# Three tiles for rows of B in a Mamba and mixture-of-experts layer, with every step's place chosen anew

## What is computed

```python
h0 = layernorm(x)
xs, z = split(h0 @ in_proj_w.T)                    # 512 features each
xc = silu(causal_conv4(xs) + conv_b)
B, C, d = split(xc @ x_proj_w.T)                   # 16, 16 and 1 values a token
dt = softplus(d);  A = -exp(A_log)                 # A: 512 x 16
# over time, for each feature and each n of 16:
h[n] = exp(dt * A[:, n]) * h[n] + dt * B[n] * xc
y = sum_n C[n] * h[n]
x = x + ((y + D * xc) * silu(z)) @ out_proj_w.T
t = layernorm(x)
w, e = top2(softmax(t @ router_w.T + router_b))    # 2 of 8 experts
x = x + sum_k w[k] * (t @ expert_weights[e[k]])
```

## Time and profile before

| | us |
|---|---|
| median of 3 runs | 2778.48 |
| lowest and highest | 2769.5, 2797.36 |
| profiled execution, its own time | 2768.58 |
| its span, first to last instruction | 2766.5 |
| busy PE, DVE | 2313.6, 2273.5 |
| busy POOL, ACT | 1809.8, 1488.8 |

### The profile page before, as it was taken

One profiled execution on the slowest core, in us unless ns is written; L12 is line 12 of the kernel. 1 busy time (PEld: TensorE's weight loads), 2 busy tenths in 40 slices (PEclk: granted clock), 3 DMA queues, 4 the chain that ended last, 5 costly groups with the idle time before them and its releaser, 6 DMA issues.

```text
span 2766.5 us, 34600 instructions
## 1 busy us (share of the span) xinstructions
PE 2313.6 (84%) x9510; PEld 1336.4 (48%) x9510; DVE 2273.5 (82%) x3144; ACT 1488.8 (54%) x2417; POOL 1809.8 (65%) x1418
## 2 busy tenths in 40 slices
PE   5668777798979889798988889798987989798886
PEld 2435353554545454454545455454544545454432
DVE  3899999899899989898999979898899989888200
ACT  3554646465654746565564656556574656545221
POOL 2556767557576767768676766767686676669442
PEclk8878788799989999898999989899999999999998
DMA  3873412324233434435343444534444353456875
GB/s 121 277 264 95 155 59 58 96 77 134 73 122 112 138 118 116 132 111 145 114 146 103 123 132 109 145 104 148 115 121 128 105 155 107 126 153 183 217 209 152
DMA packets 192570, 366.27 MB, mean 132 GB/s; under 512 B 22912, under 2 KB 22912, under 8 KB 192384
## 3 DMA queue, kind: packets, MB, share of 16 engines
q1 hardware_dynamic: 144272, 263.26, 29.8%
q0 software_dynamic: 28672, 67.13, 11.3%
q10 hardware_dynamic: 19440, 33.69, 3.4%
HBM read 212.73 MB, written 151.26 MB: 132 GB/s over the span
## 4 chain that ended last, share of the span: by engine, by line
PE 33%; DVE 24%; POOL 15%; issue 14%; ACT 11%; DMA 2%; SPq 0%; DVEq 0%; POOLq 0%; another core or an unknown queue 0%; ACTq 0%
DVE h L1069 13%; PE bank L1240 12%; PE bank L1244 11%; POOL u L785 9%; PE bank L1255 7%; DVE acc L1077 6%; ACT bank L930 4%; PE bank L1235 3%; DVE xc L1100 2%; ACT L930 1%; ACT xc L982 1%; POOL row_scratch L872 1%; PE bank L1317 1%; POOL row_scratch L870 1%; POOL x_out L885 1%
## 5 line engine op out<-in xcount | busy, mean ns | idle before, releaser
L785 POOL TENSOR_TENSOR u<-xc,b_ring 128x1024 f32<-128x1024 f32 x512 | 1230.2, 2419 | 644.4 <-DVE h L1069 434.9
L930 ACT ACTIVATE bank<-dt,neg_a 128x512 f32<-128x512 f32 x1024 | 701.6, 689 | 799.4 <-DVE h L1069 686.4
L1255 PE MATMUL bank<-ident,h 128*128 128x128 f32 x4096 | 643.4, 292 | 240.5 <-DVE h L1069 137.5
L1255 PEld LDWEIGHTS bank<-ident,h 128*128 128x128 f32 x4096 | 511.2, 150 | 559.4 <-DVE h L1069 206.2
L1069 DVE TENSOR_TENSOR_SCAN h<-bank,h_last,u 128x512 f32<-128x512 f32 x512 | 652.7, 1276 | 93.8 <-ACT bank L930 52.6
L1077 DVE SCALAR_TENSOR_TENSOR acc<-bank,ct,acc 128x512 f32<-128x512 f32 x960 | 696.5, 726 | 7.7 <-PE bank L1255 7.5
L1069 DVE TENSOR_TENSOR_SCAN h<-bank,u 128x512 f32<-128x512 f32 x512 | 620.9, 1215 | 92.8 <-ACT bank L930 54.6
L1240 PE MATMUL bank<-w_exp,xeT 128*128 x764 | 381.6, 623 | 43.5 <-ACT xeT L1038 20.5
L1244 PE MATMUL bank<-w_exp,xeT 128*128 x764 | 362.1, 596 | 0.0
L1240 PE MATMUL bank<-xnT,w_in 128*128 128x512 f32 x512 | 257.4, 627 | 9.2 <-DVE acc L1077 3.6
L1244 PE MATMUL bank<-xnT,w_in 128*128 128x512 f32 x512 | 242.3, 596 | 0.0
(11 more groups left out here) (149 smaller groups left out, 2193.1 us busy)
## 6 DMA issues: line engine op xcount, KB each, us to landing
b_ring<-b_scratch SPq DMA_DIRECT2D x256, 256.0 KB
xe<-row_scratch SPq DMA_DIRECT2D x165, 256.0 KB
result_scratch<-ye SPq DMA_DIRECT2D x165, 256.0 KB
row_scratch<-x_out ACTq DMA_DIRECT2D x32, 1024.0 KB, 5.4
x<-in_x SPq DMA_DIRECT2D x66, 256.0 KB, 4.3
x_scratch<-x SPq DMA_DIRECT2D x64, 256.0 KB, 2.4
xn<-in_x SPq DMA_DIRECT2D x62, 256.0 KB, 3.7
x_out<-x_scratch SPq DMA_DIRECT2D x44, 256.0 KB, 4.6
```

Of the source, the lines that this page charges most:

```text
L785: nc.gpsimd.tensor_tensor(out=u[:, at:at + 2, :], in0=xc[:, half, 2 * k:2 * k + 2, :], in1=b_ring[:, n % ROWS:n % ROWS + 1, :].to_broadcas ...
L930: nc.scalar.activation(decay_bank(j, n, c)[:], dt[:, half, :], ACT.Exp, scale=neg_a[:, c, n:n + 1]).then_inc(decay_ready, 1)
L1255: last = nc.tensor.transpose(ps[:, k * P:(k + 1) * P], tile(k), ident[:])
```

## The change

ROWS goes from 2 to 3. The tile of a row is now chosen by its number over all blocks (16 rows don't divide by 3), in the request and in `u`. `load_b` leaves the head of the slots and becomes a step with a place of its own, in a new table B_ROWS, 15 for the rows of this pass and one for row 0 of the next block. All other tables have new places; the steps themselves and their waits are as they were. In the diff, lines of tables that the text doesn't name are left out.

```diff
--- before.py
+++ after.py
@@ -26,7 +26,7 @@
     BATCHES = TOKENS // SEQ
     LN_EPS = 1e-5
     EPS = 1e-10
-    ROWS = 2
+    ROWS = 3
     UR = 4
     XP = 2 * N + 1
     TOP = 2
@@ -60,123 +60,127 @@
     ROW_ZEROS = 32
 
     COMBINE = {
...
-        "gather": [8.8, 12.29, 29.08, 31.46, 41.89, 47.71, 54.7, 60.67],
...
+        "gather": [15.12, 17.05, 30.19, 32.14, 42.99, 48.01, 53.62, 60.57],
...
     }
     POST = {
-        "load_res": [2.18, 3.07, 4, 5.1],
-        "y_T": [4.43, 4.52, 4.87, 4.87],
-        "y_skip": [5.75, 5.85, 7.57, 7.79],
-        "y_gate": [6.67, 6.71, 10.4, 10.55],
-        "out_project": [10.75, 11.89, 14.71, 15.84],
...
-        "residual": [12.98, 15.77, 16.24, 18.77],
-        "rstd2": [19.16, 21.93],
...
-        "norm2": [18.17, 18.67, 22.72, 24.06],
...
-        "router": [18.97, 21.04, 25.63, 27.28],
...
-        "gate_weights": [37.72],
-        "rank": [35.14],
-        "row_of": [38.98],
...
-        "scatter": [48.38, 52.16, 59.82, 62.85],
+        "load_res": [1.66, 3.92, 8.45, 8.63],
+        "y_T": [4.81, 4.81, 4.83, 4.9],
+        "y_skip": [5.78, 5.9, 7.96, 8.28],
+        "y_gate": [8.01, 9.19, 10.19, 11.31],
+        "out_project": [10.75, 11.67, 12, 16.16],
...
+        "residual": [12.95, 14.45, 17.62, 19.91],
+        "rstd2": [18.09, 25.08],
...
+        "norm2": [19.53, 20.65, 24.77, 25.1],
...
+        "router": [19.37, 22.67, 26.41, 28.79],
...
+        "gate_weights": [38.47],
+        "rank": [38.34],
+        "row_of": [39.91],
...
+        "scatter": [49.1, 55.25, 59.55, 66.53],
     }
     PREP = {
-        "load_x": [0, 0.96, 8, 8.36],
...
-        "norm_apply": [10.01, 10.14, 18.01, 18.99],
-        "norm_T": [9.89, 9.9, 16.62, 17.49],
...
-        "silu_x": [38.14],
...
-        "xp_project": [38.68],
-        "xp_evict": [40.96],
...
-        "b_scale": [43.97],
-        "b_store": [50.38],
+        "load_x": [0, 3.7, 7.42, 8.24],
...
+        "norm_apply": [11.14, 11.43, 18.88, 19.14],
+        "norm_T": [10.02, 11.31, 18.31, 18.35],
...
+        "silu_x": [39.93],
...
+        "xp_project": [38.39],
+        "xp_evict": [42.44],
...
+        "b_scale": [48.39],
+        "b_store": [55.58],
     }
     EXPERTS = {
...
-        "rows_load": [6.06, 7.2, 8.67, 20.56, 28.6, 34.67, 38.35, 39.62, 47.1, 50.39, 60.45, 62.19],
...
-        "expert_end": [14.16, 16.45, 20.89, 28.62, 33.06, 35.44, 42.33, 49.08, 56.19, 60.91, 62.38, 68.25],
-        "expert_evict": [17.5, 19.88, 25.42, 34.04, 37.55, 39.98, 51.57, 57.23, 60.02, 64.58, 67.09, 71.31],
-        "rows_store": [17.96, 19.22, 34.78, 36.85, 38.91, 46.01, 53.05, 56.99, 61.37, 64.93, 65.49, 73.82],
...
+        "rows_load": [4.09, 6.76, 9.47, 18.9, 27.93, 30.67, 37.96, 43.43, 46.7, 50.29, 59.19, 60.15],
...
+        "expert_end": [14.75, 17.61, 21.83, 29.4, 34.15, 36.83, 43.33, 50.38, 56.79, 61.3, 62.43, 69.25],
+        "expert_evict": [18.43, 19.98, 24.15, 35.52, 38.95, 42.62, 53.13, 58.59, 60.46, 66.77, 68.73, 74.52],
+        "rows_store": [16.92, 19.51, 32.79, 39.28, 40.82, 55.88, 58.41, 59.3, 64.87, 67.3, 70.28, 73.12],
     }
     EXPERTS_LATE = {
-        "late_rows_load": [3.82, 4.26, 4.29, 4.39, 9.49, 12.64, 16.21, 17.84, 21.26, 25.9, 27.45, 29.91, 30.44, 37.02, 39.03, 42.58, 45.34, 46.59, 48.78, 53.56, 54.22, 56.16, 56.2],
-        "late_rows_T": [7.93, 9.04, 9.12, 11.54, 17.77, 18.54, 21.06, 21.53, 25.39, 27.97, 28.35, 31.68, 36.22, 38.05, 41.48, 44.27, 45.94, 50.51, 53.54, 55.96, 57.56, 59.45, 62.5],
...
+        "late_rows_load": [4.28, 4.32, 4.52, 4.87, 14.14, 15.01, 16.4, 16.83, 21.47, 24.84, 26.4, 26.99, 31.61, 33.1, 37.49, 39.73, 46.34, 47.29, 50.18, 54.92, 54.98, 55.47, 55.93],
+        "late_rows_T": [8.08, 9.09, 11.25, 13.25, 16.13, 17.77, 20.05, 21.53, 25.59, 26.08, 28.35, 32.67, 36.42, 38.05, 42.18, 43.44, 46.33, 50.51, 54.81, 55.12, 56.68, 58.01, 60.69],
...
     }
     EXPERTS_END = {
...
     }
     POST_END = {
-        "end_load_res": [0.7, 7.69, 8.52, 9.85],
...
-        "end_store_x1": [3.27, 9.96, 12.1, 15.35],
...
-        "end_rank": [47.69],
+        "end_load_res": [0.1, 1.7, 8.6, 8.77],
...
+        "end_store_x1": [2.97, 9.4, 10.55, 13.54],
...
+        "end_rank": [49.89],
         "end_row_of": [66.9],
...
         "end_scatter": [66.9, 66.9, 66.9, 66.9],
     }
     COMBINE_LATE = {
...
-        "near_gather": [56.5, 58.66, 60.91, 61.75, 63.81, 65.23, 66.3, 66.67],
...
+        "near_gather": [56.62, 58.74, 60.54, 64.14, 64.44, 65.21, 66.26, 66.9],
...
+    }
+    B_ROWS = {
...
     }
     PAIRS = [(i, k) for i in range(Q) for k in range(TOP)]
     INDEX = {"gather": PAIRS, "late": [(i, k) for k in range(TOP) for i in range(Q)], "conv": [(c, k) for c in range(C) for k in range(EDGE)]}
@@ -262,6 +266,10 @@
         side = combine_in(j) + post_in(j) + prepare_in(j) + experts_in(j)
         if j in NEW_GROUP:
             side = [(6, ("new_group", NEW_GROUP[j]))] + side
+        if scan:
+            side = side + [(at, ("load_b", n + 1, 0)) for n, at in enumerate(B_ROWS["load_b"])]
+        if do_prep:
+            side = side + [(B_ROWS["next_load_b"][0], ("load_b", 0, 1))]
         if j == 0:
             side = side + [(2 * i + 1, ("zero_rows", i)) for i in range(ROW_ZEROS)]
         if j == 1:
@@ -274,11 +282,6 @@
         steps = []
         for at in range(N * C):
             n, c = at // C, at % C
-            if c == 0:
-                if scan and n + 1 < N:
-                    steps.append(("load_b", n + 1, 0))
-                elif do_prep and n + 1 == N:
-                    steps.append(("load_b", 0, 1))
             if scan:
                 steps += [("u", n, c // 2)] * (c % 2 == 0) + [("decay", n, c), ("scan", n, c)]
             k = at - C - LAG
@@ -672,7 +675,8 @@
                         n, of = s[1], j + s[2]
                         sync.wait_ge(b_stored, 16 * (of + 1))
                         wait(sync, u_ready, (of * N + n - ROWS + 1) * C // 2)
-                        sync.dma_start(b_ring[:, n % ROWS, :], b_dram[(half + s[2]) % 2, n:n + 1, :].to_broadcast([P, T])).then_inc(b_loaded[n % ROWS], 16)
+                        row = of * N + n
+                        sync.dma_start(b_ring[:, row % ROWS, :], b_dram[(half + s[2]) % 2, n:n + 1, :].to_broadcast([P, T])).then_inc(b_loaded[row % ROWS], 16)
                     elif s[0] == "rows_load":
                         g, at, tile = tile_of(s[1])
                         if at == 0:
@@ -775,15 +779,16 @@
                         nc.gpsimd.tensor_tensor(out=shift1[:, two], in0=mean[:, two], in1=rstd[:, two], op=ALU.mult).then_inc(shift_ready, 1)
                     elif s[0] == "u":
                         n, k = s[1], s[2]
+                        row = j * N + n
                         if k == 0:
-                            pool.wait_ge(b_loaded[n % ROWS], 16 * (j * (N // ROWS) + n // ROWS + 1))
+                            pool.wait_ge(b_loaded[row % ROWS], 16 * (row // ROWS + 1))
                         if n == 0 and k == 0:
                             pool.wait_ge(xc_ready, (j + 1) * C)
                         g = n * 2 + k
                         at = 2 * (g % 2)
                         wait(pool, scanned, j * N * C + 2 * (g - 1))
                         nc.gpsimd.tensor_tensor(out=u[:, at:at + 2, :], in0=xc[:, half, 2 * k:2 * k + 2, :],
-                                                in1=b_ring[:, n % ROWS:n % ROWS + 1, :].to_broadcast([P, 2, T]), op=ALU.mult).then_inc(u_ready, 1)
+                                                in1=b_ring[:, row % ROWS:row % ROWS + 1, :].to_broadcast([P, 2, T]), op=ALU.mult).then_inc(u_ready, 1)
                     elif s[0] == "conv_edge" and half == 0:
                         base = j // 2 * EDGE_STEPS
                         if j == 0:
```

More of the change, by code:

```diff
@@ L62, in mamba_moe_kernel @@
     COMBINE = {
-        "fetch": [3.46, 12.94, 35.73, 39.01],
-        "gather": [8.8, 12.29, 29.08, 31.46, 41.89, 47.71, 54.7, 60.67],
-        "store": [27.39, 35.74, 61.02, 66.51],
+        "fetch": [4.82, 14.74, 38.7, 41.01],
+        "gather": [15.12, 17.05, 30.19, 32.14, 42.99, 48.01, 53.62, 60.57],
+        "store": [31.86, 34.91, 61.37, 66.64],
     }
     POST = {
-        "load_res": [2.18, 3.07, 4, 5.1],
-        "y_T": [4.43, 4.52, 4.87, 4.87],
-        "y_skip": [5.75, 5.85, 7.57, 7.79],
@@ new lines, in mamba_moe_kernel @@
+        "out_project_end": [10.81, 11.99, 14.14, 17.66],
+        "residual": [12.95, 14.45, 17.62, 19.91],
+        "rstd2": [18.09, 25.08],
+        "store_x1": [11.18, 13.47, 16.85, 18.99],
+        "norm2": [19.53, 20.65, 24.77, 25.1],
+        "norm2_T": [17.95, 20.59, 24.38, 25.51],
+        "norm2_evict": [19.67, 21.68, 26.07, 27.75],
+        "router": [19.37, 22.67, 26.41, 28.79],
+        "gate_logits": [22.43, 25.93, 26.99, 31.31],
+        "gate_top": [32.43],
+        "gate_exp": [35.34],
@@ new lines, in mamba_moe_kernel @@
+        "project": [20.66, 23.39, 26.91, 31.42],
+        "project_end": [22.5, 27.15, 29.85, 33.11],
```

(30 more changed lines are left out.)

101 lines of the change are left out of this document (37 added, 64 removed).

## The result

The changed kernel takes 2802.25 us (2799.18 to 2807.81, 15 runs) against 2769.5 us (2759.64 to 2797.36, 15 runs) of the kernel before (the three runs shown above are among these): ratio 1.0118, 95% interval 1.0103 to 1.0133. It is slower, by more than this measurement's uncertainty, and above the whole predicted range (2706 to 2792). The profiled execution has a span of 2802.3 us, 35.8 more than before.

A forecast was written before the change was run, and what follows sets the result against it. DVE's recurrence, 64 sequential scans, was taken to bound each 160 us pass, with 20.8 us idle to win or lose. Terms -8 - 10 - 16 - 12 + 14 - 3 = -35 us gave 2744 us, range 2706 to 2792.

The forecast's parts named there:

- Edits not named here swap neighbours whose producers are done ... I count 0: All moved places without their own price: could go either way, counted as 0.
- gate_weights after u(9,1): Mid-pass: POOL's 7.4 us chain delays u(10,0), silu_x sinks behind xp_project; +1.2 us a block, +14, from 0 to +35.
- the new wait near place 40: Sign on DVE, mid-pass: a new wait of 1 to 3 us would confirm the cost term.
- rival (a): Whole pass: each removed wait is replaced by the next dependence, about -13 us stays; 2765 us, chance 0.27.
- (b): Middle of the pass: POOL's chain delays u(10,0), silu_x holds PE; 78 us cost, 2807 us, chance 0.12.
- y_T ahead of expert_end: Before y_skip in even blocks: PE transposes go ahead of 1.9 us of expert product; -10 us, from 0 to -14.
- norm2 after rstd2: DVE's 1.47 us wait near place 20: ACT no longer stands for POOL's rstd2; -1.0 a block, -12, 0 to -18.
- y_gate and gathers: POOL before out_project: later gathers let u(2,1) start 1.6 us earlier; -1.3 a block, -16, from 0 to -35.
- Block 15: Row requests ahead of rows_load: first DVE stall goes, some 3 us of the second stay; -8, 0 to -14.
- The last stretch: After the last pass: end_load_res 1 requested ahead of store_x1, against DVE's 11.31 us wait; -3, from +8 to -11.
- the first 48 and little more: Sign of rightness: POOL's waits for rows fall to this, SyncE's for u from 930 us to under 200.
- In blocks 1 to 14 I price this at nothing: Third tile and request places: 0 on DVE, row waits covered by the scan ring; bound about 20 us.

The follow-up runs named there:

- experiment 1: Changed kernel with row_of's ranks kept in their PSUM bank, so each product reads one operand from PSUM: 2769.04 us, ratio 1.0003.
- Experiment 5: Kernel before with gate_weights at 38.47, row_of at 39.91, ranks in PSUM and the row-number cast replaced by a second sum: 2783.39 us, ratio 1.0052.
- experiment 3: Kernel before with gate_weights at 38.47, row_of at 39.91 and the ranks kept in PSUM: 2810.23 us, ratio 1.0139.
- Experiment 11: Changed kernel with ranks in PSUM, plus the request for row 3 at place 4.2 instead of 4.88: 2768.13 us, ratio 1.0004.
- experiment 2: Kernel before with only gate_weights moved from 37.72 to 38.47 and row_of from 38.98 to 39.91: 2817.11 us, ratio 1.0194.
- experiment 6: Changed kernel with gate_weights alone back at 37.72, row_of left at 39.91: 2816.65 us, ratio 1.0177.

## Why the prediction was wrong

It was wrong in sign. The sum had -35 us; the span rose by 35.8. Two things failed: a term was missing, and the gains did not add.

**The missing term.** The step that failed is "Edits not named here swap neighbours whose producers are done ... I count 0", under which row_of's move from 38.98 to 39.91 fell, and beside it "gate_weights after u(9,1)", priced at +14 us, 0 to +35, where row_of appears only as time that passes. I costed that move by its semaphores only and said that row_of's "small operations lie between". What runs showed in its place: row_of now falls under u, and its products stand for 53.3 us. Taking the second SBUF operand away gives 37.7 us of span back (2802.3 to 2764.6), more than the whole 35.8; the products get 53.5 shorter, the cast 12.7 longer.

The term as I had defined it, POOL's chain and silu_x, did not come. In experiment 1 DVE waits at most 0.2 us at each of the places 38 to 41, where before it waited 1.23 at 38 and 0.27 at 41 (even blocks): the new wait near place 40 that was to confirm the term is absent. Experiment 5 has the size that I had named, 0.0052 x 2769 = 14 us or +1.2 us a block, but not the cause: no scan waits for u(10,0) there, silu_x is at its old place, and what is paid is row_of's own time beside ACT's wait. The size was right by chance.

The trace of before had shown the effect, in rows that I didn't read. The first instruction of new_group turns 8 numbers a partition, SBUF to SBUF, and its duration spreads by a factor of ten on the same shape:

```profile
L1194 DVE TENSOR_SCALAR tiles_i<-fill x9: 145/1010/1469, 501.8 to 2652.9; 128x8 int32<-128x8 int32 x9
```

The first six of the nine take 0.58 to 1.47 us, and each ends within 0.04 us of the end of a u; the last three, 0.15 to 0.17 us, have no u beside them.

The Trainium skill, SBUF — State Buffer, SBUF: two separate sides, states the rule: VectorE and GpSimd share a pair of SBUF ports as an exclusive lock, held for a whole instruction, and a VectorE instruction takes it when it runs in a two-port mode or, against a GpSimd instruction that reads SBUF, when it has two SBUF inputs. The trace agrees: the products end with u (1406.83 and 1406.79). The Trainium skill, VectorE: DVE Perf Modes, The perf-mode tier table, gives a doubled rate and all modes, the two-port ones among them, to copies and tensor_scalar of float32 in SBUF, and only the single mode to tensor_reduce. That fits the cast, held up to 2877 ns in experiment 3, and the sum in its place, never over 222; which mode ran is in no trace.

**The gains did not add.** With the stand gone the change stands at 1.0003 (experiment 1). That is nearest to rival (a), gains hidden one behind another, which I had at 2765 and 0.27; but of the 13 us that (a) kept, block 15's share did not stay either. The block terms asked for 2.5 us less in an even block (-1.4 -1.3 -1.0 +1.2) and 1.1 in an odd one. In experiment 1 DVE waits 15.84 us in an even block for 17.89 (mean of blocks 4 to 14), but 14.01 in an odd one for 12.98, and the cast takes 0.8 us of each; passes 7 to 13 of the changed kernel are 158.8 to 164.7 us long, which I had named as a sign of (a) or (b). Term by term, in the changed kernel:

- y_T ahead of expert_end, -10: in the six even blocks 4 to 14 the waits before y_skip fell from 14.1 to 5.8 us (now 0.96 to 0.98 each), -8.3, and in the last stretch from 8.1 to 4.6. Right in its place.
- norm2 after rstd2, -1.0 a block: place 20 went from 1.47 to 0.50. Right in its place, and 25 fell from 0.99 to 0.12; but place 24 went from 0.45 to 1.23 and 26 from 0 to 0.62.
- y_gate and gathers, -1.3 a block: 0.95 us at place 11 and 0.86 at 18 are gone, place 12 has 1.70 for 2.30 (even blocks); a new wait for out_project at 19 takes 1.92. Of -1.3, -0.5 is left.
- Block 15, -8: it is 4.2 us longer, and 3.6 longer in experiment 1, where nothing of the products stands. The first stall went, as said. The second was forecast at "some 3 us" and is 7.17. Experiment 11 takes it away and gains nothing, so even the right size would have been hidden.
- Unnamed places, 0: besides row_of, the waits at 63 (1.55 us) and at 61 (0.71) are gone, and waits of 2.50 at place 0 and 1.25 at 46 have come.
- The last stretch, -3: 204.2 us for 203.4.

Block 15 in the changed kernel, for the earlier trace rows: the SyncE queue, POOL, DVE.

```profile
2457.59 0.34 SPq L696 DMA_DIRECT2D xn<-row_scratch  x1
2458.03 0.38 SPq L679 DMA_DIRECT2D b_ring<-b_scratch  x1
```

```profile
2461.93 4.68 POOL L790 TENSOR_TENSOR u<-xc,b_ring 128x1024 f32<-128x1024 f32 x2 [11.27 <-DMA b_ring<-b_scratch]
```

```profile
2464.37 1.28 DVE L1074 TENSOR_TENSOR_SCAN h<-bank,h_last,u 128x512 f32<-128x512 f32 x1 [7.17 <-POOL u L790]
```

The request for row 3 does stand right behind the rows_load, as said, and u is there 3.9 + 2.4 us after it, which I had at 3.5 + 2.3. But it goes out 32 us into the pass (2458.0 less 2426), where the forecast of 2420.9 was 26 us into it: I took the rows_load at its old time less one stall, and it now waits longer.

**Rows.** POOL's waits for rows came as said ("the first 48 and little more": 49.3 and 11.3), SyncE's for u did not: 627.9 us, not under 200. "In blocks 1 to 14 I price this at nothing" was wrong both ways: on the old order tile and requests cost 0.6%, on the new one they carry 70.8 us. They had no price of their own; it depends on where the rest lies.

**Rival (b)** named this place, and its time, 2807, is near the one measured. Its mechanism isn't what happened: no scan waits for u(10,0), and at places 38 to 41 experiment 1 shows nothing that silu_x's slip costs, where (b) had 78 us. It was near by chance.

In sum: the two places alone with their stand 1.0194 and without it 1.0052; the whole change with its stand 1.0118 and without it 1.0003 or, with the second sum, 0.9988.

## What to carry to other kernels

When a change moves an instruction in time, ask of it not only what it waits for but what runs beside it: here a small VectorE operation with two SBUF operands, or a cast from SBUF to SBUF, cost what was left of GpSimd's instruction, and no wait in the profile says so. Look at min/median/max of the small instructions before pricing a move; here a spread from 0.2 to 2 us on a fixed shape was contention. And ask what the instruction covered where it stood: row_of had run in the shadow of a wait for ACT. An operation that is held was better made harmless (one operand in PSUM, a sum for a cast) than moved back, and where it would wait for the same GpSimd instruction anyway, the stand is free.

## What the runs showed of the hardware

- VectorE's product of 128 x 32 numbers with both operands in SBUF takes 0.18 to 0.24 us alone, and up to 2.4 us beside POOL's u of 2.35 us (changed kernel), up to 3.6 beside a gather and the u behind it (experiment 2). It ends 0.05 to 0.06 us after u. With one operand in PSUM it takes 0.19 us at most in every run.
- A cast of 128 x 8 numbers, SBUF to SBUF, is held too: 0.17 us alone, up to 2.88 in experiment 3 and, once, 3.66 in experiment 6. A sum from SBUF to SBUF (128 x 64 to 128 x 8) is not: 0.22 us in every run.
- The profile books the stand as busy time of VectorE: 2318.6 us for 2273.5 with the same 3144 instructions. A comparison of waits alone finds nothing here: DVE's idle time fell from 493 to 484 us.
